# Self-attention in a decoder layer: another cut of scores, values and fillers on one core

## Chip, cores and metric

The kernel runs on one core of a Trainium2 chip. The metric is the device time of one execution in microseconds (us), as the median of several runs. A core has TensorE (matrix products, written PE in profiles), VectorE (DVE), ScalarE (ACT), GpSimd (POOL) and SyncE (SP), which here issues transfers. Each engine runs its own list of instructions in order; semaphores tie them together.

## What is computed

A pre-norm decoder layer on x of 8 batches x 512 rows x 512 columns: self-attention, then cross-attention with a router, then a block on selected rows. The change is in self-attention alone, which is this (cut from the reference; B is 8 batches here, windows of 512 rows, H = 16 heads of HD = 64, G = 128; x is layer-normed ahead of it):

```python
h = x * jax.lax.rsqrt(jnp.mean(x * x, axis=-1, keepdims=True) + EPS) * norm_w
q, k, v = (proj(w_q), proj(w_k), proj(w_v))
ll = jnp.einsum('bhnqd,bhnkd->bhnqk', qw, kw) * scale
ll = jnp.where(cm, ll, NEG).reshape(B, H, S, W)
scores = (jnp.einsum('bsd,do->bso', h, scorer_w) + scorer_b)[..., 0]
_, idx = jax.lax.top_k(scores, G)
...
attn = jax.nn.softmax(jnp.concatenate([ll, lg], axis=-1), axis=-1)
...
return x + jnp.einsum('bse,ed->bsd', o, w_out)
```

A row that is among the 128 of highest score is seen twice by every later query, so its probability counts double. The kernels need no second set of keys for it: each key gets a weight of 1 or 2, found by counting how many rows rank above it.

## The kernel before

`self_attention` works batch by batch (a loop of eight), and inside a batch by pairs of heads, eight of them. `attention_plan` writes the order of a batch as one list, and every engine walks that list and takes the entries that concern it. q, k and v are products of numbers split into a high and a low part (`product`, L577 to L579: high x high, low x high, high x low, for four chunks, so twelve matmuls of 512 columns each; lines of `product` carry the projections' time). All split weights lie in SBUF.

A pair is five *units* (`unit_blocks`), each with 512 columns of causal scores: two with the last 128 queries of a head, two with 128 + 384 columns, one with 256 + 256. For each unit:

- TensorE, L661: `q_both` (high and low part of q one above the other, 128 rows) times `k_twice`; L664 (or L657): 64 rows of q high times `k_lo`; L665: a bf16 matmul that adds the causal mask. One bank of PSUM, `s_bank`, for the unit, two in turn.
- VectorE, L530 or L525: the negated largest score of each row. ScalarE, L405: the exponential, into `probs`.
- TensorE, L673: four transposes of `probs` into `pt_bank`. VectorE, L538: copy to `probs_t`.
- TensorE, L688: probabilities as the stationary operand, values (64 columns and one of weights, `VW` = 65) as the moving one, in fp32, where one product is two instructions in the trace. The 65th column collects the sum of the row. VectorE, L552 and L553: reciprocal of it and product, into `o_norm`.

When a pair is through, L697 turns `o_norm` with four transposes and ScalarE, L413, copies it to `o_t`. The scores of unit g stand one unit ahead of the transposes of g - 2 and the values of g - 3. The four half pieces of the next pair's q and k are spread through the pair. The eight value projections stand at the start of a batch, the output projection (`out`, L712, 64 instructions of 512 columns) at its end, with nothing beside them but their own evacuation. Statistics, the dot with the scorer, ranks and the transposes of the next batch's h (`ht`, L605) are spread through the batch.

## Time and profile before

| | us |
|---|---|
| median of three runs | 2407.46 |
| lowest and highest | 2406.68, 2407.98 |
| the profiled execution, its own time | 2402.29 |
| its span, first to last instruction | 2400.2 |
| TensorE busy | 2236.6 (93%) |
| VectorE busy | 1331.6 (55%) |
| ScalarE busy | 889.6 (37%) |
| GpSimd busy | 387.6 (16%) |

The profile is of one execution. A busy engine is one with an instruction in work; of TensorE the ends are modelled and overlap, so a duration of one matmul is longer than its share of the engine's time, and the distance between two starts says what one costs. A line number in a row is one of the kernel's source. "idle ... <-X" is the time that the engine stood still before the instruction, and who released it.

### The profile page before, as it was taken

The numbers are of one execution on the slowest core, as the hardware profiler recorded it, in microseconds if no ns is written. First come the engines' busy times: TensorE is split into PE (matmuls) and PEld (weight loads), VectorE is DVE, ScalarE is ACT, GpSimd is POOL, SyncE is SP. The second block draws the span as 40 slices with busy tenths as digits, with TensorE's granted clock in tenths as the row PEclk, the third lists the DMA queues.
The fourth block names the chain that finished last, engine by engine and source line by source line (L and its number), as shares of the span: only waits on it lengthen the run. The fifth ranks groups of instructions, "written<-read, shape, count | busy, mean of one in ns | idle before, by whom it ended". The sixth has DMA issues, their size and how long they took to land. (4 is left out here: it accounts for less than half of the span.)

```text
span 2400.2 us, 35872 instructions
## 1 busy us (share of the span) xinstructions
PE 2236.6 (93%) x12029; PEld 1677.1 (70%) x12029; DVE 1331.6 (55%) x3145; ACT 889.6 (37%) x1765; POOL 387.6 (16%) x637
## 2 busy tenths in 40 slices
PE   3999999999999999999999999996889989978899
PEld 3776777677677677757767866783778878864543
DVE  4574367177257536716734752771688878845500
ACT  3442344144144234414414432441665555513210
POOL 2100000010010000001001000101665555520000
PEclk9999999999999999999999999998988888759999
DMA  5000000100100000010010001003012311141000
GB/s 184 1 1 27 27 1 10 45 1 1 54 1 1 26 29 1 10 45 1 1 54 1 1 18 36 1 1 101 24 36 78 132 56 55 53 150 53 1 0 18
DMA packets 46136, 80.23 MB, mean 33 GB/s; under 512 B 10067, under 2 KB 10067, under 8 KB 45448
## 3 DMA queue, kind: packets, MB, share of 16 engines
q1 hardware_dynamic: 45320, 75.85, 9.2%
q8 instruction: 103, 1.69, 0.3%
q0 software_dynamic: 640, 2.10, 0.2%
q14 instruction: 73, 0.60, 0.1%
HBM read 60.11 MB, written 17.83 MB: 32 GB/s over the span
## 5 line engine op out<-in xcount | busy, mean ns | idle before, releaser
L405 ACT ACTIVATE probs<-s_bank,nmax 128x512 f32<-128x512 f32 (+3 forms) x512 | 249.4, 525 | 421.4 <-DVE nmax L530 294.3
L530 DVE TENSOR_REDUCE nmax<-s_bank 128x1 f32<-128x512 f32 (+2 forms) x384 | 185.3, 511 | 305.8 <-PE s_bank L665 302.1
L688 PE MATMUL o_bank<-vals,probs_t 128*128 128x65 f32 x2560 | 322.1, 269 | 0.0
L688 PEld LDWEIGHTS o_bank<-vals,probs_t 128*128 128x128 f32 x2560 | 311.0, 192 | 1.4 <-DVE probs_t L538 1.4
L712 PE MATMUL pj_bank<-w_o,o_t 128*128 128x512 f32 x512 | 223.5, 597 | 6.0 <-ACT o_t L413 6.0
L538 DVE COPY probs_t<-pt_bank 128x512 f32<-128x512 f32 x320 | 218.1, 682 | 3.6 <-PE pt_bank L673 3.6
L673 PE MATMUL pt_bank<-ident,probs 128*128 128x128 f32 x1280 | 194.1, 274 | 0.0
L712 PEld LDWEIGHTS pj_bank<-w_o,o_t 128*128 128x128 f32 x512 | 97.2, 191 | 127.6 <-issue 127.6
L664 PE MATMUL s_bank<-k_lo,q_both 64*128 64x512 f32 (+3 forms) x448 | 184.9, 413 | 0.0
L319 POOL TENSOR_TENSOR idle<-ones 128x4 f32<-128x4 f32 x41 | 8.2, 199 | 1064.7 <-DMA probs<-in_x 1062.6
L383 ACT ACTIVATE vals<-pj_bank,twice 128x512 f32<-128x512 f32 x64 | 44.0, 688 | 342.0 <-PE pj_bank L579 336.5
L661 PE MATMUL s_bank<-k_twice,q_both 128*128 128x512 f32 (+3 forms) x448 | 166.9, 373 | 0.0
L514 DVE SCALAR_TENSOR_TENSOR q_both<-pj_bank,q_both 64x512 fp32r<-64x512 f32 x128 | 88.2, 689 | 141.5 <-ACT q_both L392 138.9
L1268 PEld LDWEIGHTS x_o_bank<-vx,p_t 77*128 77x128 f32 x1024 | 146.2, 221 | 16.5 <-issue 8.2
L1268 PE MATMUL x_o_bank<-vx,p_t 77*128 77x33 f32 x1024 | 141.7, 298 | 3.6 <-DVE att L1150 3.6
L664 PEld LDWEIGHTS s_bank<-k_lo,q_both 64*128 64x128 f32 x448 | 81.8, 183 | 85.5 <-issue 72.1
L570 DVE TENSOR_TENSOR probs<-pj_bank,probs 128x512 f32<-128x512 f32 x32 | 22.1, 692 | 213.8 <-PE pj_bank L712 207.6
L673 PEld LDWEIGHTS pt_bank<-ident,probs 128*128 128x128 f32 x1280 | 135.7, 141 | 0.0
L577 PE MATMUL pj_bank<-wv_hi,ht_hi 128*128 128x512 f32 x256 | 104.2, 407 | 23.0 <-ACT vals L383 10.0
L1022 POOL TENSOR_TENSOR e<-e,fill 128x616 f32<-128x616 f32 x64 | 95.5, 1491 | 143.3 <-DVE fill L1135 143.3
L1254 PE MATMUL e_bank<-qk_bd,xl_t 128*128 128x308 f32 x256 | 95.8, 505 | 23.7 <-DVE e L1129 23.1
L665 PE MATMUL s_bank<-causal_b,ident_b 128*128 128x128 bf16 x512 | 117.7, 230 | 0.0
(267 smaller groups left out, 4225.8 us busy)
## 6 DMA issues: line engine op xcount, KB each, us to landing
xb<-in_x SPq DMA_DIRECT2D x9, 1024.0 KB, 5.4
xt<-x SPq DMA_DIRECT2D x36, 256.0 KB, 2.9
probs<-in_x SPq DMA_DIRECT2D x32, 256.0 KB, 2.6
x<-probs SPq DMA_DIRECT2D x32, 256.0 KB, 2.0
am<-in_L_ffn_attention_mask SPq DMA_DIRECT2D x8, 1024.0 KB, 5.2
out<-x SPq DMA_DIRECT2D x32, 256.0 KB, 2.1
w_sb<-in_L_ffn_w SPq DMA_DIRECT2D x2, 4096.0 KB, 20.7
o_t<-in_L_attn_w_v SPq DMA_DIRECT2D x2, 1024.0 KB, 9.5
```

The lines of the kernel that those rows point to most:

```text
L405: ins = nc.scalar.activation(probs[:, i % 2, c0:c0 + nk], s_bank[i % 2][:, c0:c0 + nk], ACT.Exp, bias=nmax[:, i % 4, n:n + 1])
L530: ins = nc.vector.tensor_reduce(nmax[:, i % 4, n:n + 1], s_bank[i % 2][:, c0:c0 + nk], AX.X, ALU.max, negate=True)
L538: nc.vector.tensor_copy(probs_t[:, i % 2, :], pt_bank[slot][:, :]).then_inc(ts_ready, 1)
L577: nc.tensor.matmul(out, lhs_hi, rhs_hi, start=start, stop=False)
L661: nc.tensor.matmul(s_bank[slot][:, c0:c0 + nk], *high, start=True, stop=False)
L664: nc.tensor.matmul(s_bank[slot][:, c0:c0 + nk], *low, start=False, stop=False)
L665: ins = nc.tensor.matmul(s_bank[slot][:, c0 + nk - P:c0 + nk], ident_b[:, :], causal_b[:, :], start=False, stop=True)
L673: ins = nc.tensor.transpose(pt_bank[slot][:, P * j:P * j + P], probs[:, i % 2, P * j:P * j + P], ident[:, :])
L688: ins = nc.tensor.matmul(o_bank[slot][:, o0:o0 + VW], probs_t[:, i % 2, c0 + P * kt:c0 + P * kt + P], vals[:, kt, 2 * p + h, :], start=(kt ...
L712: ins = nc.tensor.matmul(pj_bank[slot][:, :], o_t[:, c, P * i:P * i + P], w_o[:, c, :], start=(c == 0), stop=(c == NPAIR - 1))
L1254: ins = nc.tensor.matmul(e_bank[:, c, 0:CH * SK], xl_t[:, (i // 2) % 2, P * k:P * k + P], qk_bd[:, n.par, k].rearrange("p h k -> p (h k)") ...
L1268: ins = nc.tensor.matmul(o_bank[:, VX * h:VX * h + VX], p_t[:, i % 2, h // CH, P * (h % CH):P * (h % CH) + P], vx[:, n.par, 2 * CH * (i % ...
```

## The change

Self-attention is written anew around *slots*: 24 a batch (`NG`), three groups (slots) to a pair. Both heads are worked on in each group.

- **Groups.** `score_parts`: group 0 is queries 384 to 511 with 512 keys, group 1 queries 256 to 383 with 384 keys, group 2 queries 128 to 255 with 256 keys and queries 0 to 127 with 128 keys. A group has one unit per head, in `s_bank[h]`.
- **Scores.** q and k are kept as high and low parts of 128 rows, head 0 in rows 0 to 63, head 1 in rows 64 to 127. Per part three terms (high-high, high-low, low-high), each for head 0 and then head 1 with 64 rows. q carries the sign minus. The causal matmul is gone.
- **Mask and weight.** A bias tile (`bias`: causal plus minus ln 2 for keys that count double) is made once a batch from the ranks, by a second transpose (`tw`) and four adds (L710). VectorE's new operation (L654) reads scores from PSUM, adds the bias, writes the sum to `probs` in SBUF and keeps the row's smallest. ScalarE makes the exponential in place and sums the row (`den`). GpSimd takes the reciprocal of the sum as a power (L479), and scales the row in place (L484).
- **Transposes** of `probs` as before, twenty a pair; ScalarE copies the high part (`pt_hi`), VectorE makes the low part (`pt_lo`).
- **Values stationary.** `vals` holds high and low parts, 128 columns a head, as stationary operand; the transposed probabilities are the moving one with 512, 384, 256 and 128 columns, high and low. The result is the turned output: ScalarE copies 64 rows to `o_t`, VectorE adds the other 64. `o_norm`, its transposes and the reciprocals on VectorE are gone.
- **Fillers.** `PIECES` lays half projections (six matmuls of q, k or v; half of an output projection) into slots. "-" means the batch before, "+" the next one. So the output of batch b stands in slots 2 to 6 of batch b + 1, and v0 to v3, q0, q1 and k0 of the next batch in slots 19 to 23. On TensorE a slot is: scores, value products (every third slot), transposes of the group before, pieces.
- **Weights of q and k** no longer all stay in SBUF: they are split once, stored to memory (`wqk_split`) and fetched pair by pair, 1 MB for each pair of each batch, by SyncE.
- **Loop.** Batch 0, batch 7 and what hangs over it are written out; the loop runs over the six between.

```diff
-UNITS = 5
-NU = NPAIR * UNITS
+NG = 3 * NPAIR
+NU = 2 * NG
...
+PIECES = {0: "v3b k1a", 1: "k1b", 2: "q2a q2b o0a- o0b-", 3: "k2a k2b o1a- o1b-", 4: "o2a-", 5: "o2b- o3a-",
+          6: "o3b- q3a q3b", 7: "k3a k3b", 8: "q4a q4b v4a", 9: "v4b k4a k4b", 10: "v5a", 11: "v5b q5a q5b",
+          12: "k5a k5b v6a", 13: "v6b", 14: "q6a q6b v7a", 15: "v7b k6a k6b", 17: "q7a q7b k7a",
+          18: "k7b ht0+ ht1+ ht2+ ht3+", 19: "v0a+ v0b+", 20: "q0a+ q0b+ v1a+ v1b+", 21: "k0a+ k0b+ v2a+",
+          22: "v2b+", 23: "q1a+ q1b+ v3a+"}
...
+    for g in range(NG):
+        at.append(("s", g, g))
+        at += [("m", 2 * g + j, g) for j in range(2)]
+        at += [("t", 2 * g + j, g + 1) for j in range(2)]
+    for p in range(NPAIR):
+        at += [("pv", 2 * p + h, 3 * p + 4) for h in range(2)]
...
+def score_parts(g):
+
+    return ([(3, 0, 512)], [(2, 0, 384)], [(1, 0, 256), (0, 256, 128)])[g % 3]
...
+                if kind == "m":
+                    slot, parts = i % 4, score_parts(i // 2)
+                    k = len(parts)
+                    pl.wait_ge(p_ready, n.count(NU, i + 1))
+                    nc.gpsimd.tensor_tensor(rden[:, slot, 0:k], den[:, slot, 0:k], minus[:, 0:k],
+                                            ALU.pow).then_inc(rden_ready, 1)
...
+                        ins = nc.gpsimd.tensor_scalar(probs[:, slot, c0:c0 + nk], probs[:, slot, c0:c0 + nk],
+                                                      rden[:, slot, k:k + 1], 1.0, ALU.mult, ALU.mult)
+                    ins.then_inc(norm_ready, 1)
...
+                    for k, (t, c0, nk) in enumerate(score_parts(g)):
+                        ins = nc.vector.tensor_tensor_reduce(probs[:, slot, c0:c0 + nk], s_bank[h][:, c0:c0 + nk],
+                                                             bias[:, mask_cols(t)], 1.0, 3.0e38, ALU.add,
+                                                             ALU.min, nmax[:, slot, k:k + 1])
...
-                        for h, t, c0, nk in unit_blocks(u):
-                            queries, rows = slice(P * t, P * t + P), head_rows(h)
-                            high = (q_both[:, p % 2, h, queries], k_twice[:, p % 2, h, 0:nk])
-                            low = (q_both[rows, p % 2, h, queries], k_lo[rows, p % 2, 0:nk])
...
-                            ins = nc.tensor.matmul(s_bank[slot][:, c0 + nk - P:c0 + nk], ident_b[:, :], causal_b[:, :],
-                                                   start=False, stop=True)
...
+                    wait(pe, max_ready, n.count(NU, 2 * i))
+                    for t, c0, nk in score_parts(i):
+                        cols, queries = slice(c0, c0 + nk), slice(P * t, P * t + P)
+                        for step, (a, b) in enumerate(((q_hi, k_hi), (q_hi, k_lo), (q_lo, k_hi))):
+                            for h in range(2):
+                                rows = head_rows(h)
+                                ins = nc.tensor.matmul(s_bank[h][:, cols], a[rows, p % 2, queries],
+                                                       b[rows, p % 2, 0:nk], start=(step == 0), stop=(step == 2))
...
-                                ins = nc.tensor.matmul(o_bank[slot][:, o0:o0 + VW],
-                                                       probs_t[:, i % 2, c0 + P * kt:c0 + P * kt + P],
-                                                       vals[:, kt, 2 * p + h, :], start=(kt == 0), stop=(kt == nk // P - 1))
...
+                    for k in range(TT):
+                        for part in (pt_hi, pt_lo):
+                            ins = nc.tensor.matmul(
+                                o_bank[h][:, P * k:S],
+                                vals[:, k, p, 2 * h:2 * h + 2, :].rearrange("p s d -> p (s d)"),
+                                part[:, h, 4 * k:3 * k + TT, :].rearrange("p t q -> p (t q)"),
+                                start=(k == 0 and part is pt_hi), stop=(k == TT - 1 and part is pt_lo))
```

TensorE before, one unit in the middle of a pair: scores, transposes of an earlier unit, values of a still earlier one.

```order
L661 MATMUL s_bank<-k_twice,q_both 128x128
L664 MATMUL s_bank<-k_lo,q_both 128x128
L665 MATMUL s_bank<-causal_b,ident_b 128x128
L661 MATMUL s_bank<-k_twice,q_both 128x384
L664 MATMUL s_bank<-k_lo,q_both 128x384
L665 MATMUL s_bank<-causal_b,ident_b 128x128
L673 MATMUL pt_bank<-ident,probs 128x128 x4
L688 MATMUL o_bank<-vals,probs_t 128x65 x4
```

TensorE after, a slot with the last group of a pair, and behind it the pieces of that slot (q of a later pair; `wqk` is its fetched weights).

```order
L777 MATMUL s_bank<-k_hi,q_hi 128x256 x2
L777 MATMUL s_bank<-k_lo,q_hi 128x256 x2
L777 MATMUL s_bank<-k_hi,q_lo 128x256 x2
L777 MATMUL s_bank<-k_hi,q_hi 128x128 x2
L777 MATMUL s_bank<-k_lo,q_hi 128x128 x2
L777 MATMUL s_bank<-k_hi,q_lo 128x128 x2
L786 MATMUL pt_bank<-ident,probs 128x128 x6
L761 MATMUL pj_bank<-ht_hi,wqk 128x512
```

All score matmuls of a group now stand in one block of one form, where products of 128 and of 64 rows and the mask took turns; "x2" are the two heads.

TensorE before, the values of one unit are the last row above. After, the values of one head (every third slot has two such blocks), then the transposes of the group before:

```order
L799 MATMUL o_bank<-pt_hi,vals 128x512
L799 MATMUL o_bank<-pt_lo,vals 128x512
L799 MATMUL o_bank<-pt_hi,vals 128x384
L799 MATMUL o_bank<-pt_lo,vals 128x384
L799 MATMUL o_bank<-pt_hi,vals 128x256
L799 MATMUL o_bank<-pt_lo,vals 128x256
L799 MATMUL o_bank<-pt_hi,vals 128x128
L799 MATMUL o_bank<-pt_lo,vals 128x128
L786 MATMUL pt_bank<-ident,probs 128x128 x8
```

The products of five units have become two blocks of eight wide ones.

GpSimd after, the two units of group 1 and the first of group 2 (`units` holds sums and reciprocals, `fixed` constants); before, GpSimd had nothing at all inside a pair.

```order
L479 TENSOR_TENSOR units<-units,fixed 128x1
L482 TENSOR_TENSOR units<-fixed 128x1
L484 TENSOR_SCALAR probs<-probs,units 128x384
L479 TENSOR_TENSOR units<-units,fixed 128x2
L482 TENSOR_TENSOR units<-fixed 128x1
L484 TENSOR_SCALAR probs<-probs,units 128x256
L484 TENSOR_SCALAR probs<-probs,units 128x128
```

A step on GpSimd now stands between ScalarE's exponential and TensorE's transpose, for each of the 48 units of a batch.

## Rows read from the trace of the kernel before

**Rows 1.** The page: busy us, share of the span, instructions of each engine.

```profile
PE 2236.6 (93%) x12029; PEld 1677.1 (70%) x12029; DVE 1331.6 (55%) x3145; ACT 889.6 (37%) x1765; POOL 387.6 (16%) x637
```

**Rows 2.** Busy by stretch (PE, PEld, DVE, ACT, POOL), clock, DMA share, GB/s.

```profile
652.00:853.00 201.00, 197.31 (x1077) 146.99 (x1076) 107.67 (x254) 71.46 (x133) 11.20 (x26) 1.00 0.05 17
1656.00:2400.00 744.00, 648.00 (x3401) 494.35 (x3401) 440.56 (x1062) 302.54 (x698) 282.82 (x396) 0.85 0.18 59
```

**Rows 3.** Instructions of one line: ns min/median/max, first and last start us.

```profile
L506 DVE COPY vals<-twice x8: 218/228/229, 48.4 to 1457.4; 128x64 f32<-128x64 f32 x8
...
L570 DVE TENSOR_TENSOR probs<-pj_bank,probs x32: 692/692/692, 225.3 to 1654.6; 128x512 f32<-128x512 f32 x32
```

**Rows 4.** TensorE in order of time: start us, us, line, form, count.

```profile
701.20 0.48 PE L577 MATMUL pj_bank<-ht_hi,wk_hi 128*128 128x512 f32 x1
...
704.05 0.22 PE L661 MATMUL s_bank<-k_twice,q_both 128*128 128x128 f32 x1
...
705.28 0.61 PE L673 MATMUL pt_bank<-ident,probs 128*128 128x128 f32 x4
...
706.66 0.38 PE L657 MATMUL s_bank<-k_lo,q_both 64*128 64x256 f32 x1
...
707.91 0.61 PE L673 MATMUL pt_bank<-ident,probs 128*128 128x128 f32 x4
...
709.19 0.61 PE L697 MATMUL pt_bank<-ident,o_norm 128*128 128x128 f32 x4
709.55 0.48 PE L661 MATMUL s_bank<-k_twice,q_both 128*128 128x512 f32 x1
709.96 0.49 PE L664 MATMUL s_bank<-k_lo,q_both 64*128 64x512 f32 x1
710.39 0.23 PE L665 MATMUL s_bank<-causal_b,ident_b 128*128 128x128 bf16 x1
710.46 0.60 PE L673 MATMUL pt_bank<-ident,probs 128*128 128x128 f32 x4
710.90 1.00 PE L688 MATMUL o_bank<-vals,probs_t 128*128 128x65 f32 x8
711.71 0.48 PE L577 MATMUL pj_bank<-ht_hi,wq_hi 128*128 128x512 f32 x1
...
714.56 0.39 PE L661 MATMUL s_bank<-k_twice,q_both 128*128 128x512 f32 x1
...
715.37 0.61 PE L673 MATMUL pt_bank<-ident,probs 128*128 128x128 f32 x4
...
716.62 0.31 PE L661 MATMUL s_bank<-k_twice,q_both 128*128 128x128 f32 x1
...
717.95 0.61 PE L673 MATMUL pt_bank<-ident,probs 128*128 128x128 f32 x4
```

**Rows 5.** TensorE in order of time, end of batch 7: the output projection.

```profile
1626.74 27.73 PE L712 MATMUL pj_bank<-w_o,o_t 128*128 128x512 f32 x64 [0.75 <-ACT o_t L413]
```

**Rows 6.** Groups, forms apart: count, busy us, mean ns, idle before, releaser.

```profile
L405 ACT ACTIVATE probs<-s_bank,nmax 128x512 f32<-128x512 f32 x128 | 88.1, 689 | 126.7 <-DVE nmax L530 126.7
...
L530 DVE TENSOR_REDUCE nmax<-s_bank 128x1 f32<-128x128 f32 x128 | 37.4, 292 | 149.0 <-PE s_bank L665 147.3
...
L437 DVE CUSTOM_DVE_ANT_0 junk<-xb,sw 128x512 bf16<-128x512 f32 x36 | 24.9, 692 | 0.9
...
L437 DVE DVE_READ_ACCUMULATOR2_ANT score<- 128x1 f32 x36 | 3.0, 82 | 0.0
...
L353 POOL TENSOR_SCALAR probs<-probs,res_now 128x512 f32<-128x512 f32 x32 | 24.7, 772 | 0.0
...
L319 POOL TENSOR_TENSOR idle<-ones 128x4 f32<-128x4 f32 x41 | 8.2, 199 | 1064.7 <-DMA probs<-in_x 1062.6 <-POOL res_next L335 2.1
...
L1477 POOL TENSOR_TENSOR r<-r,f_half 128x1 f32<-128x1 f32 x4 | 2.2, 553 | 0.3
```

**Rows 7.** DMA issues: count, KB each, median us to landing.

```profile
xb<-in_x SPq DMA_DIRECT2D x9, 1024.0 KB, 5.4
```

More of the change, by code:

```diff
@@ L40 @@
 NEG = -1e30
-UNITS = 5
-NU = NPAIR * UNITS
-VW = HD + 1
 class Tally:
@@ new lines, in projected, with turned, run, period @@
+        def projected(eng, key, n):
+            eng.wait_ge(pj_ready, proj_ring.count(key, n))
+            return pj_bank[proj_ring.slot(key, n)]
+        def turned(eng, key, n):
+            eng.wait_ge(pt_ready, turn_ring.count(key, n))
+            return pt_bank[turn_ring.slot(key, n)]
+        def run(order, work, eng, tally=None, per=0, extra=None):
+            def period(n):
+                slots = [[a for a in order if a[3] == s] for s in range(NG)]
+                for s, items in enumerate(slots):
+                    for kind, i, off, _ in items:
+                        if not n.fixed or 0 <= n.index + off < B:
+                            work(kind, i, n.ahead(off))
+                    if extra and n.fixed and n.index == 0:
+                        extra(s)
+            period(Round(0, 0))
+            with eng.Fori(0, B - 2) as j:
+                if tally:
+                    with tally.loop(j, per, B - 2):
+                        period(Round(j, 1))
+                else:
+                    period(Round(j, 1))
+            period(Round(0, B - 1))
+            period(Round(0, B))
@@ L415, in _ @@
+            work("vb", 1, zero)
+            work("vb", 2, zero)
+            work("qb", 1, zero)
+            tail = ("ht",) + tuple(k for k in PIECE_KINDS)
+            mixed = [a for s in range(NG) for a in act_order(s, tail)]
+            run(mixed, work, act, extra=lambda s: split(SPLIT_IN_SLOT[s]) if s in SPLIT_IN_SLOT else None)
         @block.vector
@@ L573, in _, with bank_for @@
+            work("vb", 1, zero)
+            rank(zero, 2)
+            rank(zero, 3)
+            work("vb", 2, zero)
+            work("tw", 0, zero)
+            work("bias", 0, zero)
+            work("qb", 1, zero)
+            mixed = [a for s in range(NG) for a in dve_order(s)]
+            run(mixed, work, dv, done, TT + TT + 2 * TT + 1,
+                extra=lambda s: split(SPLIT_IN_SLOT[s]) if s in SPLIT_IN_SLOT else None)
         @block.tensor
         def _(pe):
+            def bank_for(ring, banks, taken, key, n):
+                count = ring.count(key, n)
+                if not isinstance(count, int) or count > 2:
+                    pe.wait_ge(taken, count - 2)
+                return banks[ring.slot(key, n)]
```

927 lines of the change are left out of this document (499 added, 428 removed).

## The prediction

> **What bounds the kernel now.** I read the page's first lines, then the busy time by stretch, then TensorE in order of time inside one pair of heads. TensorE is busy for 2236.6 us, 93% of a span of 2400.2 [rows 1]. Busy share alone proves little, because matmuls are pipelined, so I went to the stretches. One batch of self-attention, 652 to 853 us, has TensorE busy for 197.3 of 201 us at the full granted clock, with VectorE at 107.7, ScalarE at 71.5 and GpSimd at 11.2 [rows 2]. The first value copy of a batch comes at 48.4 us for batch 0 and at 1457.4 for batch 7, so a batch takes 1409.0 / 7 = 201.3 us; the last output add starts at 1654.6, so self-attention ends at 1655.3 = 8 x 201.3 + 45 [rows 3]. TensorE sets the period. What follows, 1656 to 2400, is not touched and I keep it whole [rows 2].
>
> **A pair of heads on TensorE, before.** Starts are subtracted from starts, since the shown ends are modelled [rows 4]. One projection (12 matmuls of 512 columns): 704.05 - 701.20 = 2.85. The five score units: 0.91 (709.55 to 710.46), 0.81 (714.56 to 715.37), 1.23 (704.05 to 705.28), 1.25 (706.66 to 707.91), 1.33 (716.62 to 717.95), 5.5 together. Four transposes 0.44, so 2.2 for five. Probabilities times values 0.81, so 4.1 for five. The turn of the output 0.36. With two projections a pair takes 5.7 + 5.5 + 2.2 + 4.1 + 0.4 = 17.9; eight take 143. A batch adds eight value projections (8 x 2.85 = 22.8), the output projection, 27.7 in one row [rows 5], and twenty transposes of h and score (20 x 0.11 = 2.2). That is 196, and leaves 5 us of gaps in 201.3.
>
> **Scores.** In [rows 4] the 512-column 128-row matmul is followed after 0.41, the 64-row one after 0.43, whereas twelve like ones need 0.238 each. So each change between 128 and 64 rows costs 0.41 - 0.23 = 0.18. Before, a pair makes 16 changes: 2 in each of two units, 4 in each of three. Now all 24 score matmuls of a pair have 64 rows, in three groups, hence 6 changes, 1.1 instead of 2.9. The eight causal matmuls go too. What remains is 24 matmuls with 7680 columns, in couples that read different halves of the rows and write different banks. No row shows two such at once. Upper bound: one after the other, 7680 x 0.23 / 512 = 3.4, and a little more where short ones wait for weights (a load with a 65-column matmul takes 0.81 / 8 = 0.10), 3.8; with the changes 4.9. Lower bound: couples run together and their loads too, 1.8 + 1.1 = 2.9. I take overlapped matmuls with loads one after the other, twelve couples at 0.21 to 0.23, 2.6 + 1.1 = 3.7, since the long couples come to the same under either load rule and no operand or bank is shared. Gain 5.5 - 3.7 = 1.8 per pair, between 0.6 and 2.6.
>
> The page "TensorEngine Tiling (Array Packing)" of the Trainium skill, section Key Properties, says that a change of tiling mode drains TensorE and that different tiles can load weights and multiply in parallel. The first half agrees with the 0.18 us; no run here yet shows the second. By its text a pair's scores would take 2.9 and the whole 2127, without it 4.9 and 2259 (both among the rivals).
>
> **Values stationary.** Before, twenty fp32 products of 65 columns, forty instructions at 0.10. Now sixteen matmuls, four of each of 512, 384, 256, 128 columns: at 0.23 per 512, and not under 0.107, 4 x (0.23 + 0.17 + 0.12 + 0.11) = 2.5. Gain 1.6. The output arrives turned, so the 0.36 goes; two adds on VectorE and two copies on ScalarE take the place of ten small operations.
>
> **The rest of TensorE.** Projections, transposes of probabilities and the output projection keep their instructions; only their places change. Four transposes per batch are new (0.44). New batch: 8 x (5.7 + 3.7 + 2.2 + 2.5) = 112.8, + 22.8 + 27.7 + 2.6 = 165.9. Before, 5 us of gaps came with long uninterrupted pieces; now slots change kind oftener and slot 16 has no filler, so I add 6: **172 us a batch**. Had the gaps gone altogether it would be 166.
>
> **What the other engines get.** VectorE per pair: eight reductions that also add the bias, 2560 columns; six low parts, 2560; two adds; low parts of q, k and v: 7680 columns at (0.692 - 0.292) / 384 = 1.04 ns, 19 times a fixed 0.16, and 0.14 per head-group for the read of the accumulator and the memset [rows 6]: 12.1. Eight pairs and some 24 us per batch (ranks, dot, statistics, h, bias, out: about thirty operations of 0.7 and their reads) make 121 of 172. ScalarE has the same 7680 columns, exponentials at 0.689 per 512 [rows 6] and copies at less, some 10.2 per pair, and the sums of the rows are new on it, 0 to 0.3 each: about 95. GpSimd gets the division: per unit a power of one column 0.55, a tiny operation 0.2, a scaling 0.77 for 512 columns [rows 6], less for shorter, 9.3 per pair, some 10.5 with hand-overs, and its old 11.2: 95 of 172. None is the bound by sum. The weights of q and k come back from memory, 1 MB per pair; such a load lands in 5.4 us [rows 7], is issued two pairs ahead, and costs nothing unless SyncE stands at an output for over 20 us.
>
> **The chain in a slot.** From the end of a group's scores: VectorE 0.83 for the first head, ScalarE 0.7 to 1.0, GpSimd twice 1.5 to 1.7, with hand-overs of about 0.1 and a possible late VectorE (0.3): 5.3 to 6.3 before the last transpose can start. TensorE has the rest of its slot and the next scores meanwhile: in a slot without output pieces six transposes 0.66 and three half projections 4.1, then scores 1.1, so 5.9 at the least, up to 6.5. The next scores also wait until VectorE has read both banks, 1.7 after the last ones, well inside the slot; behind that wait stands all of TensorE's work. It is just covered; slot 16 (two value products as its only filler, cover 5.0) waits about 1 us. If the cover is gone, each microsecond more costs some 6 us a batch, as slots with output, values or two queries have room.
>
> **Ends.** The first slot starts later than before's first product: ranks, bias and both splits are in line on VectorE, and pair 1's weights go out and come back (5.4 each way at most); I reckon 62 us. Batch 0 has no output pieces in slots 2 to 6 (27.7, of which the weight splits take back 3): -25. Batch 7 has no pieces for a next batch, 20.6 on TensorE, of which the chain keeps a third: -14. After slot 23 of batch 7: last transposes, value products, then the output unhidden, 36. Together 59, where it was 45. Self-attention: 8 x 172 + 59 = 1435, against 1655: -220. Span 2400.2 becomes 2180; the execution lasts 2 us longer, 2182, and the median of the runs is 5 above that of the profiled one (2407.5 against 2402.3): **2187 us**.
>
> **Rivals.**
> - *Heads one after the other.* Scores 4.9 per pair: batch 165.9 + 9.6 + 6 = 181, 8 x 181 + 59 = 1507, time 2259. For it: nothing in the trace overlaps 64-row matmuls. Against: the pieces that could collide are separate.
> - *The chain binds.* ScalarE's sum or the two GpSimd units take 8 us instead of 6: 188 a batch, 1563, time 2315. For it: cover of a few tenths only, strict order on VectorE, with statistics and dot, four operations of 0.7 with their reads each, in two slots.
> - *Everything is cheaper*: loads overlap too (2.9 per pair) and gaps stay 5: 164.5 a batch, 2127.
> - *Slower than before: GpSimd becomes the bound*, at the division in L479 to L484. 48 units a batch at u us plus 12: this passes 199.5 (where 8 batches and the ends make the old 1655) at u = 3.9, against 1.5 to 1.8 worked out. At u = 4.5 it is 228 a batch, 1883 in all, time 2635. For it: no row has GpSimd and VectorE this busy together. Against: more than twice every row.
> - *The change does not spread*: if the output pieces did not find work to lie beside, nothing is lost, since they cost TensorE the same in either place; the gain rests on fewer TensorE microseconds and not on spreading.
>
> The page "SBUF — State Buffer" of the Trainium skill, section Summary: rules for kernel authors, says that VectorE with two SBUF inputs blocks a GpSimd operation that reads SBUF, whole instructions long. The new score and low-part operations read PSUM and one SBUF tile, so by it only ranks and dot could hold the division; if the rule held for all, it would be the fourth rival. GpSimd's scaling took 0.772 in the mean of its 32 runs, which lay beside reductions from PSUM [rows 6].
>
> **Chances.** Forecast (2150 to 2225) 0.50; heads in turn (2225 to 2290) 0.20; chain 0.14; cheaper 0.11; GpSimd bound 0.05, of which 0.04 slower. Range: from the cheaper case, 2125, to between the second rival and the third, 2300; outside remain about 0.05 below and 0.13 above. Under 0.2%, about 5 us, could not be told from no change: 0.01. Faster 0.95, slower 0.04.
>
> **What would show it.** Batch period near 172 between the first value copies; score couples that start under 0.05 us apart (right) or 0.23 apart (in turn); 0.18 at six places per pair instead of 16; a 16-matmul value product of 2.5; TensorE still busy over 90%. Idle time before the transposes of probabilities with GpSimd as releaser, over 1 us in most slots, would speak for the chain. GpSimd above 150 us per batch would speak for the fourth. The forecast is wrong in kind if the granted clock falls below 1.00 within slots, or if TensorE waits for a weight load.

## The result, and the profile after the change

The changed kernel takes 2168.04 us (median of four runs, 2167.51 to 2178.75) against 2407.39 for the kernel before, run beside it: a ratio of 0.9022, 95% interval 0.9009 to 0.9035. The forecast was 2187, its range 2125 to 2300, so the time was 19 us off, 8% of the 239 us gained. The profiled execution took 2167.51 us, its span is 2165.8.

The page of the changed kernel, engines first, then the largest gap of TensorE (busy, mean ns, idle before, releaser), and the load of the split weights (count, KB, us to landing):

```profile
span 2165.8 us, 34295 instructions
PE 1954.0 (90%) x10249; PEld 1450.7 (67%) x10249; DVE 1286.0 (59%) x3621; ACT 983.9 (45%) x2471; POOL 951.5 (44%) x1900
...
L786 PE MATMUL pt_bank<-ident,probs 128*128 128x128 f32 x1280 | 189.5, 286 | 61.3 <-POOL probs L484 57.3
...
wqk<-wqk_split SPq DMA_DIRECT2D x63, 1024.0 KB, 4.9
```

Against [rows 1] TensorE is busy 282.6 us less (2236.6 - 1954.0) and the span is 234.4 shorter: TensorE lost work, and some 48 us of idle time came in. 57.3 us of that has one name, transposes of probabilities that wait for GpSimd. GpSimd went from 387.6 to 951.5 us and is still only 44% busy.

Busy time by stretch, the changed kernel: one middle batch, and all that follows self-attention (columns as in [rows 2]):

```profile
728.00:896.00 168.00, 160.31 (x849) 117.12 (x848) 103.44 (x317) 83.47 (x220) 83.21 (x186) 0.98 0.20 70
1422.70:2165.80 743.10, 649.07 (x3401) 495.80 (x3401) 440.16 (x1062) 302.60 (x698) 282.94 (x396) 0.85 0.18 59
```

The part behind self-attention is what it was (743.1 here, 744 in [rows 2], both cut by hand at the ends). So the whole gain is in self-attention, which ends at 1422.5 instead of 1655.3. A mark that comes once a batch gives the period. VectorE of the changed kernel in order of time, the bias for the next batch:

```profile
216.21 1.72 DVE L710 TENSOR_TENSOR bias<-row_s,causal 128x128 f32<-128x128 f32 x4
...
1229.34 1.12 DVE L710 TENSOR_TENSOR bias<-row_s,causal 128x128 f32<-128x128 f32 x3
```

Six periods lie between: (1229.34 - 216.21) / 6 = **168.9 us a batch**, where the kernel before took 201.3 and the forecast said 172.

Where TensorE's time went inside a pair, in order of time, two stretches of one batch:

```profile
759.61 0.50 PE L799 MATMUL o_bank<-pt_hi,vals 128*128 128x512 f32 x1
...
762.22 1.06 PE L786 MATMUL pt_bank<-ident,probs 128*128 128x128 f32 x8
...
766.64 0.39 PE L777 MATMUL s_bank<-k_hi,q_hi 64*128 64x256 f32 x2
...
767.48 0.76 PE L786 MATMUL pt_bank<-ident,probs 128*128 128x128 f32 x5
...
775.15 0.50 PE L777 MATMUL s_bank<-k_hi,q_hi 64*128 64x512 f32 x2
775.49 0.40 PE L777 MATMUL s_bank<-k_lo,q_hi 64*128 64x512 f32 x2
775.72 0.41 PE L777 MATMUL s_bank<-k_hi,q_lo 64*128 64x512 f32 x2
776.06 0.88 PE L786 MATMUL pt_bank<-ident,probs 128*128 128x128 f32 x6
...
783.06 0.44 PE L777 MATMUL s_bank<-k_hi,q_hi 64*128 64x384 f32 x2
...
783.78 0.50 PE L799 MATMUL o_bank<-pt_hi,vals 128*128 128x512 f32 x1
```

The sixteen value matmuls take 762.22 - 759.61 = 2.61. The three groups of scores take 0.91 (775.15 to 776.06), 0.72 (783.06 to 783.78) and 0.84 (766.64 to 767.48), together **2.47 us a pair** where [rows 4] had 5.5 and the forecast 3.7. A row "x2" at L777 is a couple, one product of each head: the couples of 512 columns follow one another after 0.34, 0.23 and 0.34. 0.23 is the time of one such matmul alone, so the second costs nothing, its weight load included. The two 0.34 are the 0.23 and 0.11 for the change of form (from matmuls with 128 rows to ones with 64, or back) at either side. The matmul just outside is followed later too: the last 512-column one of a projection before a group after 0.32 instead of 0.23 (782.74 to 783.06). The 2.47 do not hold this 0.09, which comes before 20 of the 24 groups of a batch, some 1.8 us; in the sum below it is among the gaps.

With the measured terms a batch is 8 x (5.7 + 2.5 + 2.2 + 2.6) + 22.8 + 27.7 + 2.6 = 157.1. The period is 168.9, so 11.8 us are gaps, not 6. The largest, TensorE in order of time again:

```profile
790.75 0.28 PE L777 MATMUL s_bank<-k_hi,q_lo 64*128 64x128 f32 x2
794.86 0.90 PE L786 MATMUL pt_bank<-ident,probs 128*128 128x128 f32 x3 [3.84 <-POOL probs L484]
796.21 0.90 PE L786 MATMUL pt_bank<-ident,probs 128*128 128x128 f32 x3 [0.45 <-POOL probs L484]
796.76 0.78 PE L761 MATMUL pj_bank<-ht_hi,wqk 128*128 128x512 f32 x1
797.34 0.63 PE L762 MATMUL pj_bank<-ht_hi,wqk 128*128 128x512 f32 x1
```

and what GpSimd did meanwhile:

```profile
785.44 0.20 POOL L458 TENSOR_TENSOR st<-mv,fixed 128x4 f32<-128x4 f32 x1 [4.52 <-DVE mv L601]
...
790.39 3.01 POOL L471 TENSOR_SCALAR xb<-xb,st 128x512 f32<-128x512 f32 x4
793.36 0.54 POOL L479 TENSOR_TENSOR units<-units,fixed 128x1 f32<-128x1 f32 x1
```

GpSimd works on the statistics and the scaling of the next batch's rows from 785.4 to 793.4, 8 us in one piece. ScalarE had the next group's first exponential, sum included, done at 788.03, and it waits 5.3 us for its division. TensorE waits 3.84 and 0.45, and behind the wait the projection's matmuls of 512 columns come 0.43 apart instead of 0.23. The clock in that stretch, and before and after it:

```profile
782.00:790.00 8.00, 8.00 (x47) 6.44 (x46) 6.36 (x21) 3.22 (x8) 3.77 (x11) 1.00 0.09 34
796.80:801.20 4.40, 4.40 (x13) 3.43 (x12) 3.46 (x11) 0.83 (x3) 3.69 (x7) 0.50 0.00 0
801.80:804.80 3.00, 3.00 (x20) 2.08 (x18) 1.14 (x3) 0.60 (x1) 0.00 (x0) 1.00 0.00 0
```

The granted clock is 0.50, its level of 1.2 GHz, for about eleven matmuls, which cost 0.20 more each, 2.2 together. The wait thus costs once as idle time and half as much again as slow matmuls.

### The profile page after: what moved, and what is told of

It is laid out like the page before. It is cut to its first block and busy times, and to the rows that moved or that the text cites. A ratio compares the mean times of both kernels' runs of the same rounds, so it can differ in the third digit from the quotient of the medians.

```text
span 2165.8 us, 34295 instructions
## 1 busy us (share of the span) xinstructions
PE 1954.0 (90%) x10249; PEld 1450.7 (67%) x10249; DVE 1286.0 (59%) x3621; ACT 983.9 (45%) x2471; POOL 951.5 (44%) x1900
## 5 line engine op out<-in xcount | busy, mean ns | idle before, releaser
L479 POOL TENSOR_TENSOR units<-units,fixed 128x1 f32<-128x1 f32 (+1 forms) x384 | 232.8, 606 | 644.4 <-ACT probs L544 644.3
L544 ACT ACTIVATE probs<-probs,units 128x512 f32<-128x512 f32 (+3 forms) x512 | 284.9, 557 | 492.2 <-DVE units L654 492.2
L662 DVE TENSOR_TENSOR pt_lo<-pt_bank,pt_hi 128x512 fp32r<-128x512 f32 (+2 forms) x384 | 223.0, 599 | 182.6 <-ACT pt_hi L554 181.8
L484 POOL TENSOR_SCALAR probs<-probs,units 128x512 f32<-128x512 f32 (+3 forms) x512 | 276.7, 547 | 0.0
L786 PE MATMUL pt_bank<-ident,probs 128*128 128x128 f32 x1280 | 189.5, 286 | 61.3 <-POOL probs L484 57.3
L654 DVE CUSTOM_DVE_ANT_0 probs<-s_bank,bias 128x512 f32<-128x512 f32 (+3 forms) x512 | 227.1, 487 | 13.3 <-issue 13.1
L761 PE MATMUL pj_bank<-ht_hi,wqk 128*128 128x512 f32 x512 | 221.0, 432 | 9.7 <-DMA wqk<-wqk_split 8.0
L762 PE MATMUL pj_bank<-ht_hi,wqk 128*128 128x512 f32 x512 | 207.5, 405 | 0.0
L763 PE MATMUL pj_bank<-ht_lo,wqk 128*128 128x512 f32 x512 | 207.3, 405 | 0.0
L786 PEld LDWEIGHTS pt_bank<-ident,probs 128*128 128x128 f32 x1280 | 139.6, 143 | 97.5 <-issue 61.5
L554 ACT CAST pt_hi<-pt_bank 128x512 fp32r<-128x512 f32 (+2 forms) x384 | 187.2, 504 | 36.9 <-PE pt_bank L786 35.6
L799 PE MATMUL o_bank<-pt_hi,vals 128*128 128x512 f32 (+3 forms) x512 | 160.6, 331 | 5.4 <-DVE pt_lo L662 5.4
L799 PE MATMUL o_bank<-pt_lo,vals 128*128 128x512 f32 (+3 forms) x512 | 147.9, 325 | 0.0
```

The costliest lines, as they stand in the source:

```text
L479: nc.gpsimd.tensor_tensor(rden[:, slot, 0:k], den[:, slot, 0:k], minus[:, 0:k], ALU.pow).then_inc(rden_ready, 1)
L484: ins = nc.gpsimd.tensor_scalar(probs[:, slot, c0:c0 + nk], probs[:, slot, c0:c0 + nk], rden[:, slot, k:k + 1], 1.0, ALU.mult, ALU.mult)
L544: ins = nc.scalar.activation(probs[:, slot, c0:c0 + nk], probs[:, slot, c0:c0 + nk], ACT.Exp, bias=nmax[:, slot, k:k + 1], scale=-1.0, acc ...
L654: ins = nc.vector.tensor_tensor_reduce(probs[:, slot, c0:c0 + nk], s_bank[h][:, c0:c0 + nk], bias[:, mask_cols(t)], 1.0, 3.0e38, ALU.add, ...
L662: nc.vector.tensor_tensor(dst, src, hi.bitcast(F32), ALU.subtract).then_inc(pt_taken, 1)
L761: nc.tensor.matmul(out, lhs_hi, rhs_hi, start=start, stop=False)
```

## The experiments

All were run beside the kernel before; the ratios are to it, with 95% intervals. "The changed kernel" is the one at 2168.04. Three questions were open: what makes the scores so short, what makes the gaps, and whether the cover of the slots matters at all.

**Order of the heads.** Edit: both heads' couples are written head after head.

```diff
-                        for step, (a, b) in enumerate(((q_hi, k_hi), (q_hi, k_lo), (q_lo, k_hi))):
-                            for h in range(2):
+                        for h in range(2):
+                            for step, (a, b) in enumerate(((q_hi, k_hi), (q_hi, k_lo), (q_lo, k_hi))):
```

> The changed kernel with the two loops of the score matmuls exchanged: head 0's three terms, then head 1's three, so that couples of different row halves stand next to each other only once per part instead of three times. Theory A, couples of different row halves run at the same time (the changed kernel's trace shows a couple of 512 columns every 0.23 us): a part needs five steps where it needed three, two more of 0.23, 0.17, 0.12 and 0.06, 1.15 us per pair, 9.2 per batch, and with 8 batches the execution is up to 74 us longer; where the slot was waiting for the probabilities anyway less, so 55 to 74. Theory B, the short spacing is only how the record lists them and one head is worked after the other in both orders: no change, within 5 us.

Measured: 2174.16 us (2173.8 to 2174.56), ratio 0.9034, 0.9019 to 0.9049: 6 us more, with an interval that overlaps that of the changed kernel (0.9009 to 0.9035). Theory A had said 55 to 74, theory B within 5; neither holds as it stands, and the time alone would speak for B. TensorE in order of time:

```profile
777.29 0.50 PE L777 MATMUL s_bank<-k_hi,q_hi 64*128 64x512 f32 x2
777.63 0.40 PE L777 MATMUL s_bank<-k_lo,q_hi 64*128 64x512 f32 x2
777.86 0.40 PE L777 MATMUL s_bank<-k_hi,q_lo 64*128 64x512 f32 x2
778.19 0.88 PE L786 MATMUL pt_bank<-ident,probs 128*128 128x128 f32 x6
```

The program now gives three products of head 0 and then three of head 1, and the trace still shows couples, 0.90 for the group: the fourth product of the program stands in the record beside the first, ahead of the second and third. So this run alone could not tell whether they run at the same time; it only took away theory A's premise that the order decides it.

**Same rows for both heads.** Edit: head 1's scores are taken from head 0's rows, so they are head 0's scores; number and shape of the instructions stay.

```diff
-                                rows = head_rows(h)
+                                rows = head_rows(0)
```

> The changed kernel, with head 1's score products taken from rows 0 to 63 as well (so its scores are those of head 0; nothing else is left out, and the number and shapes of all instructions stay). Both products of a couple now need the same half of the array. If the row halves run at the same time (theory: that is why three groups of scores took 2.47 us a pair in the changed kernel's trace), a couple should need twice its columns: 3 x (512 + 384 + 384) columns at 2.4 GHz are 1.6 us more per pair, 12.8 per batch, some 100 in eight batches less what the idle time of the slots gives back: 2230 to 2290 us, and the two matmuls of a couple start 0.12 to 0.23 us apart. If the two products of a couple were one after the other in the changed kernel already (rival), nothing changes: 2163 to 2173 us.

Measured: 2265.57 us (2265.23 to 2268.4), ratio 0.9419, 0.9403 to 0.9434: 97.5 us more, inside what concurrency expects. The couples, in order of time, and a group of 384 columns:

```profile
753.17 0.73 PE L777 MATMUL s_bank<-k_hi,q_hi 64*128 64x512 f32 x2
753.74 0.63 PE L777 MATMUL s_bank<-k_lo,q_hi 64*128 64x512 f32 x2
754.21 0.62 PE L777 MATMUL s_bank<-k_hi,q_lo 64*128 64x512 f32 x2
754.76 0.44 PE L786 MATMUL pt_bank<-ident,probs 128*128 128x128 f32 x2
...
777.48 0.61 PE L777 MATMUL s_bank<-k_hi,q_hi 64*128 64x384 f32 x2
...
778.73 0.50 PE L799 MATMUL o_bank<-pt_hi,vals 128*128 128x512 f32 x1
```

The group takes 754.76 - 753.17 = 1.59 instead of 0.91, and 0.47 between couples instead of 0.23, exactly double. With 1.25 for the second group (777.48 to 778.73) and 1.52 for the third (783.72 to 785.24) a pair's scores take 4.36 instead of 2.47, 15.1 more a batch. The bias comes at 225.60 and 1311.52, 181.0 a batch, 12.1 more, so 3 were given back; the waits for GpSimd in a batch fall from 5.7 to 3.1. That the two row halves compute at the same time is shown, and it is worth 97 of the 239 us. The time lands beside the 2259 that the first rival gave.

**Fewer changes of form, in the kernel before.** Edit: in the two units of a pair with 128 + 384 columns, the two blocks go part by part and not one after the other, 12 changes a pair instead of 16.

```diff
+                        if 2 <= u < 4:
+                            for part in range(3):
+                                for h, t, c0, nk in unit_blocks(u):
...
```

> The kernel before with one thing altered: in units 2 and 3 of a pair both blocks' 128-row products come first, then both 64-row ones, then both masks, so that a pair has 12 changes between 128 and 64 rows instead of 16; number and form of the matmuls are the same. Theory A, a change costs 0.18 us as the prediction read: 4 x 0.18 = 0.7 us per pair, 5.8 per batch, 46 us less, 2361. Theory B, a change costs 0.11 as in the changed kernel's trace and the rest of 0.18 was adding to the columns that the matmul just before writes: 0.44 us per pair for the changes and perhaps as much again for the distance now put between a block's products, 28 to 50 us less. Theory C, changes cost nothing and the matmuls' own latency is what the rows show: no change within 5 us. A and B are told apart by the spacing in the trace.

Measured: 2375.85 us (2373.05 to 2378.74), ratio 0.9876, 0.9859 to 0.9892: 31 us less. 4 x 64 pairs are 256 changes, so 0.12 us each, and not the 0.18 of the prediction. The trace gives the same: such a unit went from 1.23 and 1.33 [rows 4] to 0.99 (695.18 to 696.17) and 1.07 (690.01 to 691.08), 0.12 and 0.13 for each of two changes. Theory B holds as to the size. The edit also moves a block's products apart, so this is the price of a change together with that distance; the two were not separated.

**The statistics one slot earlier.** Edit: from slot 6 to slot 5 of the batch before.

```diff
-    at += [("stats", 0, -18), ("dot", 0, -16), ("score", 0, -15), ("tw", 0, -9), ("bias", 0, -1), ("res", 0, 5)]
+    at += [("stats", 0, -19), ("dot", 0, -16), ("score", 0, -15), ("tw", 0, -9), ("bias", 0, -1), ("res", 0, 5)]
```

> The changed kernel with one number altered: the statistics of the next batch stand in slot 5 instead of slot 6. In the changed kernel's trace GpSimd spends 785.4 to 793.4 on them, the division of the group of slot 7 starts behind them, TensorE waits 3.8 + 0.5 us for it in slot 8 and then runs twelve projections' matmuls at 0.43 instead of 0.23 us. Theory A, this order is what the long gap comes from: the wait goes down to under 1 us, the granted clock of the stretch back to 1.00, 5 to 6.5 us per batch in 7 batches, 35 to 45 us less, about 2125. Theory B, GpSimd's sum of work is at fault and the gap only moves to slots 6 and 7: within 10 us of the changed kernel.

Measured: 2141.97 us (2137.3 to 2146.6), ratio 0.8906, 0.8891 to 0.8921: 26 us less than the changed kernel, 30 by the spans; theory A's cause, with less than its 35 to 45. A middle batch by stretch, and what TensorE waits for in it (us, times, longest):

```profile
728.00:891.00 163.00, 158.57 (x857) 116.26 (x856) 103.45 (x318) 83.19 (x220) 83.14 (x186) 1.00 0.20 72
```

```profile
PE pt_bank L786 <- POOL probs L484: 2.4, 4, 1.0
PE pt_bank L852 <- DVE ht_lo L671: 0.9, 1, 0.9
PE o_bank L799 <- DVE pt_lo L662: 0.7, 1, 0.7
PE pt_bank L786 <- DVE pt_lo L662: 0.2, 1, 0.2
```

The first row of the changed kernel says 5.7 us, 5 times, longest 3.8; the other three are the same. The period falls to (1194.65 - 215.72) / 6 = 163.2 by the bias rows, 5.7 less: 3.3 of waits and the rest the slow matmuls, for the clock is 1.00 throughout. With the period at 163.2 the gaps are 6.1, which is what the prediction had put in: 4.2 are the waits in the rows above, and the rest is of the size of the 0.09 before 20 score groups, 1.8. Six batches give 34; batch 7, which has no statistics to do, gave nothing.

**Two slots earlier.** On the version with the shortened start, below. GpSimd then works out the residual's factors for the next batch before it has put by those of this batch, so that the last pieces get the next batch's factors.

```diff
-    at += [("stats", 0, -19), ("dot", 0, -16), ("score", 0, -15), ("tw", 0, -9), ("bias", 0, -1), ("res", 0, 5)]
+    at += [("stats", 0, -20), ("dot", 0, -16), ("score", 0, -15), ("tw", 0, -9), ("bias", 0, -1), ("res", 0, 5)]
```

> The version with the shortened start (2127 us), with the statistics of the next batch in slot 4 in place of slot 5 (slot 6 in the changed kernel). Theory: they fit where the fillers after them give cover, and the waits for GpSimd are already down to 2.4 us a batch, so the time stays within 6 us: 2121 to 2133 us. Rival: they meet the residual rows that GpSimd scales for the last output pieces in slots 4 to 6, and those delay the division: 2135 to 2160 us.

Measured: 2160.33 us (2156.9 to 2166.64), ratio 0.8974, 0.8949 to 0.9000: 34 us worse than 2126.60, and my theory was wrong. GpSimd in order of time:

```profile
752.31 0.76 POOL L493 TENSOR_SCALAR xr<-xr,res 128x512 f32<-128x512 f32 x1
755.81 0.20 POOL L461 TENSOR_TENSOR st<-mv,fixed 128x4 f32<-128x4 f32 x1 [2.73 <-DVE mv L608]
...
760.75 3.01 POOL L474 TENSOR_SCALAR xb<-xb,st 128x512 f32<-128x512 f32 x4
763.73 0.70 POOL L482 TENSOR_TENSOR units<-units,fixed 128x2 f32<-128x2 f32 x1
```

TensorE then waits 3.16 us until 767.36. The time lies at the edge of the rival's range, but its cause is not the rival's: the residual row (0.76) is done before the piece, and no load is waited for behind it. It is again the 8 us piece, in front of a group whose slot gives too little cover. Slot 5 is good and slots 4 and 6 are not. The traces show what differs: in slot 5 the piece holds back a group whose transposes stand behind the sixteen value matmuls (2.61 us), and it begins 1.4 us before that group's scores end (757.62 against 759.04). In slots 4 and 6 the group held back has no value matmuls before its transposes, and the piece begins 0.3 and 1.7 us after its scores. Which of the two counts for more was not tested.

**No division.** Edit: GpSimd's reciprocal and scaling are left out (the output lacks the division by the row sums); only the tiny hand-over operation stays.

```diff
-                    nc.gpsimd.tensor_tensor(rden[:, slot, 0:k], den[:, slot, 0:k], minus[:, 0:k],
-                                            ALU.pow).then_inc(rden_ready, 1)
...
-                        ins = nc.gpsimd.tensor_scalar(probs[:, slot, c0:c0 + nk], probs[:, slot, c0:c0 + nk],
-                                                      rden[:, slot, k:k + 1], 1.0, ALU.mult, ALU.mult)
-                    ins.then_inc(norm_ready, 1)
+                    nc.gpsimd.tensor_tensor(held_p[:, slot:slot + 1], ones[:, 0:1], ones[:, 0:1],
+                                            ALU.mult).then_inc(norm_ready, 1)
```

> The changed kernel without the division of the probabilities: the power and the scaling on GpSimd are left out, one tiny operation of 0.2 us per unit remains as the hand-over, so the attention output is not normed. The chain from scores to transposes is about 2.5 us shorter and GpSimd has 65 us less per batch. Theory A, TensorE's work sets the period and the chain is covered apart from the gaps seen (about 8 us of waiting a batch and some 3 of a lower clock): 160 or a little under per batch instead of 168, and less of a tail in batch 7, so 60 to 85 us less. Theory B, the chain sets the period in most slots: over 100 us less.

Measured: 2157.02 us (2142.44 to 2158.76), ratio 0.8963, 0.8948 to 0.8978: 11 us less. The large gain of theory B, which would have meant a chain that binds in most slots, did not come; nor did theory A's 60 to 85. The trace, of the shortest of five executions (2142.44), says why: the hand-over operation still stands behind the 8 us piece, and TensorE still waits 24.2 us for it in the whole program, where it had waited 57.3. Once a batch, in order of time:

```profile
782.12 0.87 PE L780 MATMUL pt_bank<-ident,probs 128*128 128x128 f32 x6 [2.63 <-POOL units L479]
```

Then both edits together:

> The statistics one slot earlier, as in the run that gave 2142 us, and GpSimd's reciprocal and scaling left out, as in the run that gave 2157 us (the output lacks the division by the row sums). Theory: with the statistics moved, the division is hidden under the fillers but for a few tenths per batch: 2125 to 2142 us, granted clock 1.00 in the middle batches, period 161 to 163. Rival: the chain through GpSimd still sets the end of several slots a batch, and both gains come on top of each other or more: below 2120 us.

Measured: 2130.79 us (2128.86 to 2131.58), ratio 0.8856, 0.8841 to 0.8871: 11 us below the run with the statistics moved. GpSimd's busy time in a middle batch falls from 83.1 to 21.0, TensorE no longer waits for it there, and the batch goes from 163.2 to 162.0:

```profile
728.00:890.00 162.00, 158.80 (x858) 116.25 (x857) 103.03 (x318) 82.98 (x222) 20.98 (x74) 1.00 0.21 73
```

62 us a batch of division on GpSimd cost 1.2 a batch. It is hidden, as forecast.

**The reciprocal twice.** Edit: one more reciprocal per unit, into a tile that nothing reads.

```diff
+                    nc.gpsimd.tensor_tensor(spare[:, slot, 0:k], den[:, slot, 0:k], minus[:, 0:k], ALU.pow)
                     nc.gpsimd.tensor_tensor(rden[:, slot, 0:k], den[:, slot, 0:k], minus[:, 0:k],
...
```

> The changed kernel with GpSimd's reciprocal computed twice for every unit (the first one into a spare tile that nothing reads): 0.55 to 0.71 us more on GpSimd in each of the 48 units of a batch, in the chain of each slot. GpSimd's busy time rises from 83 to some 113 us of 169 per batch, far below the bound of the fourth rival (GpSimd sets the time). Theory: the cover of most slots (fillers of 5.5 to 6 us) takes in 1.2 us more a slot only in part, so that the slots with little slack and the ones with the statistics wait longer: 3 to 12 us per batch, 2185 to 2265 us. Rival: if the chain set the end of most slots, all of 24 x 1.2 us would show: 225 us more, 2390 us. If GpSimd never mattered but for the statistics: 2168 to 2180 us.

Measured: 2224.35 us (2218.81 to 2225.18), ratio 0.9234, 0.9214 to 0.9254: 56 us more. What TensorE waits for over the whole program is 113.8 us for the divided probabilities against 57.3 in the changed kernel: the 56 again. In a middle batch:

```profile
728.00:902.00 174.00, 160.77 (x856) 117.61 (x856) 103.31 (x319) 83.82 (x220) 110.90 (x234) 0.98 0.19 68
```

```profile
PE pt_bank L788 <- POOL probs L486: 11.9, 7, 4.4
```

The chain of each slot got two units times 0.6 longer, 1.2, and there are seven waits, in six of the 24 slots, where the changed kernel has five. The batch went from 168.9 to 174.3 by the bias rows, 4.5 us per microsecond of chain; the prediction had said some 6. GpSimd at 64% of the batch sets nothing by its sum. The cover is real, and thin.

**The output pieces in two slots.** Edit: the last batch's output projection in slots 2 and 3 instead of 2 to 6, its rows' loads and stores moved along.

```diff
-PIECES = {0: "v3b k1a", 1: "k1b", 2: "q2a q2b o0a- o0b-", 3: "k2a k2b o1a- o1b-", 4: "o2a-", 5: "o2b- o3a-",
-          6: "o3b- q3a q3b", 7: "k3a k3b", 8: "q4a q4b v4a", 9: "v4b k4a k4b", 10: "v5a", 11: "v5b q5a q5b",
+PIECES = {0: "v3b k1a", 1: "k1b", 2: "q2a q2b o0a- o0b- o1a- o1b-", 3: "k2a k2b o2a- o2b- o3a- o3b-",
+          6: "q3a q3b", 7: "k3a k3b", 8: "q4a q4b v4a", 9: "v4b k4a k4b", 10: "v5a", 11: "v5b q5a q5b",
```

> The changed kernel, with the sixteen matmuls of each of the four output pieces of the last batch in slots 2 and 3 (two pieces each) in place of slots 2 to 6; loads and stores of their residual rows follow. By the prediction's rival on spreading, a piece costs TensorE the same in either place, and only slots 4 and 5, which then hold no filler, can wait for the chain of the group: one to two waits of 2 to 4 us per batch, so 8 to 45 us slower: 2175 to 2215 us, with idle time ahead of the transposes of slots 4 and 5 put down to GpSimd. If the fillers were no cover for the chain (rival), the time stays within 5 us of 2168.

Measured: 2213.58 us (2211.16 to 2226.08), ratio 0.9215, 0.9184 to 0.9246: 45.5 us more, at the upper end. In a middle batch two waits are over 1 us:

```profile
801.34 1.06 PE L786 MATMUL pt_bank<-ident,probs 128*128 128x128 f32 x6 [3.17 <-POOL probs L484]
...
818.05 0.54 PE L786 MATMUL pt_bank<-ident,probs 128*128 128x128 f32 x3 [3.58 <-POOL probs L484]
```

The first is new, in slot 6, before the transposes of the group of slot 5, which is now short; with 0.58 before the scores of slot 6 it makes up most of the change. The second is the old one of slot 8 behind the statistics. The batch takes (1261.71 - 216.61) / 6 = 174.2, 5.3 more, and TensorE executes the same instructions. These five slots instead of two are worth 45 us in this kernel.

**A shorter start.** Edit, on top of the statistics in slot 5: pair 1's weights are read and split directly, like pair 0's, and VectorE ranks before it splits the next block.

```diff
+            for k, n in enumerate("qk"):
+                sp.dma_start(first[:, 2 + k, :].rearrange("p (c e) -> p c e", c=DC), w_dram[n][:, :, P:2 * P]
+                             ).then_inc(one_in, 16)
...
-            load_pair(1)
...
             rank(zero, 0)
             rank(zero, 1)
-            split(2)
             work("vb", 1, zero)
             rank(zero, 2)
             rank(zero, 3)
             work("vb", 2, zero)
+            split(2)
...
```

> The statistics one slot earlier, and the start of the program shortened: the q and k weights of pair 1 are read and split directly, as those of pair 0 are, instead of by way of the split copy in DRAM (an 8.0 us wait for that copy in the trace), and VectorE ranks before it splits the next weights (8.9 us wait for the ranks). Theory: the first slot starts at about 53 us in place of 66 and all else stays, 13 us less than the run with the statistics moved: 2126 to 2134 us. Rival: the later split of the third weight block delays pair 2's weights, and slot 2 waits for them: 2136 to 2142 us.

Measured: 2126.60 us (2122.73 to 2132.68), ratio 0.8846, 0.8828 to 0.8863. In the changed kernel TensorE had waited 8.9 us for the ranks and 8.0 for the split copy; both waits are gone but for 0.3. The first scores in order of time:

```profile
48.45 0.50 PE L789 MATMUL s_bank<-k_hi,q_hi 64*128 64x512 f32 x2
```

They came at 66.06. Of this 17.6 us, 3 go again within batch 0. The median is 15.4 below that of the version it was built on, and this is the fastest version of the study: 41 us below the changed kernel, and the kernel before takes 13% longer.

## Why the prediction was right, by its own steps

**What bounds the kernel** was right: TensorE set the period before, and does so after (160.3 of 168 us busy). Fewer TensorE microseconds made most of the gain.

**Scores: the term was mis-sized**, 3.7 us a pair against 2.47 measured. Two prices in it were too high. Loads were taken one after the other, 2.6 for the columns, and they overlap too, 1.8: the larger part of the error. And a change of form was priced at 0.18 from the 0.41 at 709.55, a matmul that follows transposes. The same matmul behind like ones is followed after 0.32 (it starts at 714.56 in [rows 4]):

```profile
714.88 0.49 PE L664 MATMUL s_bank<-k_lo,q_both 64*128 64x512 f32 x1
```

So half of the 0.18 was not of this change. The run with fewer changes gives 0.12, and either inner side of a score group 0.11. The lower bound of 2.9 contained the 0.18: with 0.11 it is 1.8 + 6 x 0.11 = 2.5, what was measured. If the 0.09 before a group is counted as part of the change into it, that change costs 0.20; the sum has this part in the gaps. The page "TensorEngine Tiling (Array Packing)" of the Trainium skill, section Key Properties, which says that different tiles load and multiply in parallel, agrees with the trace; by its text alone the term would have been right but for my price of the change. Over 64 pairs the error is 79 us, the largest of the forecast.

**Values stationary:** 2.5 forecast, 2.61 measured. Right, as are the unchanged projections (12 matmuls in 2.9) and transposes.

**Gaps: mis-sized the other way**, 6 forecast, 11.8 measured. The step that failed is the one on the chain. It counted GpSimd's old 11.2 us a batch in a sum and let the chain have only its own operations, but on one engine in strict order an 8 us piece stands in front of a division once a batch. The piece was to be seen in the trace of before, GpSimd in order of time:

```profile
697.31 0.20 POOL L325 TENSOR_TENSOR st<-mv,eps_ln 128x4 f32<-128x4 f32 x1 [55.45 <-DVE mv L430]
...
702.33 3.04 POOL L339 TENSOR_SCALAR xb<-xb,st 128x512 f32<-128x512 f32 x4
```

697.3 to 705.4, with 55 us of idle time ahead of it that hid it. The prediction named statistics and dot on VectorE as a case for its chain rival and did not ask what they do to GpSimd. Against a cover of some 6 us that single question gives a wait of a few microseconds. By the runs it costs 5.7 a batch, of which some 2 are the slower clock behind the wait. The chain's other pinch, slot 16 with a wait of about 1 us, did not come: the transposes of its group waited 0.2.

So the period of 172 came to 168.9 out of two errors, -9.8 (8 x 1.23) and +5.8, that partly cancelled, and 0.8 from the values. That the total was near is in part luck.

**The forecast called itself wrong in kind** if the clock fell below 1.00 within slots. It did, 0.98 over a middle batch, though at one place only and not in most slots.

**The other engines** came out lower: 103, 83 and 83 us against 121, 95 and 95. The reads of the row sums on ScalarE, bounded at 0 to 0.3, took 0.187 each. A unit on GpSimd took 1.34 for 384 columns (793.36 to 794.70) and 1.75 for two blocks (796.05 to 797.80), about as forecast (1.5 to 1.8).

**Ends.** First slot at 66 (forecast 62). From the last bias row of batch 6, 1229.3, to the end of self-attention 193.2; the forecast has 158 + 36 = 194 for batch 7 and its tail. Its pieces are off in both directions. From that bias row to the last group's wait, at 1379.60, it takes 150.3 instead of 158. What follows slot 23 takes 42.9 instead of 36: TensorE waits 5.5 us for GpSimd there, which the forecast did not name, and the unhidden output is 28.6 of the rest, from

```profile
1393.94 27.73 PE L843 MATMUL pj_bank<-w_o,o_t 128*128 128x512 f32 x64 [1.40 <-DVE o_t L667]
```

Sum: 62 + 147 + 1032 + 194 = 1435 forecast, 66.1 + 150.1 + 1013.1 + 193.2 = 1422.5 measured.

**The rivals.** Heads in turn: disproved by the run with the same rows. Its 2259 lies beside the 2265.57 measured with concurrency taken away, but not by right terms: 4.9 a pair for the scores against 4.36, and gaps of 6 against 9. The chain binds: it does not in the mean, since with the statistics moved the whole division costs 1.2 a batch, but it does once a batch, and the doubled reciprocal shows how near it is. GpSimd as the bound: 83 us a batch, and no sign of it at 111. Everything cheaper: right that loads overlap (2.9 for 2.47), wrong in its gaps; with the statistics moved it is what the kernel does, 163.2 against its 164.5. **The change does not spread: this clause was wrong.** It held that output pieces cost the same in either place, which is true of their instructions, and concluded that spreading gives nothing. Put together in two slots they cost 45 us, since a slot they leave no longer covers the chain. 45 of the 239 us hang on it.

## What to carry to other kernels

Before work is put on an engine that was idle, list the longest pieces in a row that it already does and set each against the slack of the chain that it joins; its busy share tells nothing of this. Fillers are worth their cover, not only their own time: price a slot without one. A price for a switch that rests on one difference should be checked at a second place, since it is multiplied by every switch in the kernel.

## What was not expected of the hardware

- 64-row products in the two row halves ran at the same time, weight loads included: a couple of 512 columns took 0.23 us, as one alone, and 0.47 when both used the same rows. The order in which the program gave them made no difference to a group of six (0.91 and 0.90 us): with the heads in turn, the fourth product started beside the first. Why the whole was 6 us longer then stays open; the batches account for 2.5 of it (169.3 against 168.9 each).
- A change between 128-row and 64-row matmuls was worth 0.12 us where it was taken away, and showed as 0.11 at either inner side of a score group, with 0.09 more at the matmul before the group.
- After TensorE had waited 3.84 us, and 0.45 more after three transposes, the granted clock stood at 0.50 until 801.2, and matmuls of 512 columns were 0.43 apart; with waits of 1.0 at most (statistics in slot 5) it stayed at 1.00 in the middle batches.
- What stays open: of the 6 us of gaps that remain in a batch at full clock, 4.2 are waits that the trace names; that the rest is the 0.09 before the score groups rests on its size alone.
